# Depthwise 3x3 stages moved from VectorE to TensorE, fed by shifted copies that DMAs from ScalarE's queue make

## The chip, the cores and the metric

One core of a Trainium2 chip runs the whole program once. The metric is the device time of that execution in microseconds (us). Every tensor is float32. In what follows TensorE, VectorE, ScalarE, GpSimd and SyncE are the engines that a profile calls PE, DVE, ACT, POOL and SP; PEld is TensorE's weight load.

## What is computed

The input is 16 images of 256 channels, 32x32 pixels. Four blocks follow one another, each with a normalised copy of x and a residual sum. The two that matter here, cut to their core:

```python
# every block: GroupNorm of x first (groups of 8 channels), x = x + block(norm(x))
# L2: depthwise 3x3 -> BatchNorm -> ReLU -> prune -> 1x1 conv -> BatchNorm -> ReLU -> prune
y[c, h, w] = sum(dw_w[c, i, j] * xn[c, h + i - 1, w + j - 1] for i in range(3) for j in range(3))
# L3 (deformable conv): the same depthwise form, then LayerNorm over channels, GELU,
# one projection to offsets and a mask; xproj = in_w(xn); bilinear samples of xproj, out_w
```

L0 is a channel attention, L1 ("dyn") a 3x3 convolution whose weights depend on the pixel. The deformable part of L3 becomes, per image, 18 rows of tap weights (VectorE builds them), written to DRAM and read back as bands, and matmuls on those bands.

## The kernel before

Channels lie on the 128 partitions, in K = 2 halves (`k`) of 1024 pixels. Each engine has one in-order program. `run` (line 370 on) walks b from -1 to 16 and weaves three streams of work at every b: `side(b+1)` takes an image through L0, L1, dyn, L2, pw, L3, ln, om; `taps(b)` builds that image's 18 weight rows; `sample(b-1)` samples and projects the image before it in four quarters. `weave` puts the pieces in the order of hand-written numbers: `STEP` gives each stage its place (gn0 -3, L0 3, L1 19, dyn 28, L2 39, pw 48, L3 52, ln 63, om 68, sparse 76, end 80), and every `yield` names the place of what follows. So an engine's order is fixed when the program is built, and a piece that waits holds back all that stand after it.

The pieces around the change, in stage L2: VectorE takes channel statistics (`group_norm`, line 783 on), GpSimd the power, ScalarE writes the normed image into `xp`, a tile with a border of zeros (L1260). `first_tap` (L1268) makes tap 0 on ScalarE, `depthwise` (L812) the other eight on VectorE, one instruction of 1024 elements for each tap and half; L1315 is the ReLU. Then VectorE takes a maximum (L886), masks the pointwise weights (L891), TensorE multiplies (L502), ScalarE evicts (L1320), VectorE takes the next maximum (L896). Stage L3 repeats norm and depthwise, copies the normed image without its border into `acc` (L1326), TensorE makes `xproj` from it (L591), VectorE evicts that (L914); ln subtracts a mean (L921), takes a square root and a reciprocal (L925), and om makes offsets (L613, L935) and a softmax (L945 to L952, `Exp` at L1350).

A weight row u is a "build" on VectorE (L1140, L1149: 1, 3 or 5 instructions), a "sum" on TensorE (L666 to L668), a "row copy" on ScalarE (L1372, L1375) into a ring of two, and eight DMAs from SyncE (L458). `BUILD_AT` and `SUM_AT` place them. Four waits tie them:

```python
wait(ve, s_wrow, at - 1)                # build u waits for the row copy of u-2
wait(pe, s_wrow, at)                    # sum u waits for the row copy of u-1
wait(ac, s_w2[r], 16 * YB * (at // RING))  # row copy u: the DMAs of row u-2 have landed
ac.wait_ge(s_sum, at + 1)
```

A quarter of sampling is two parts of 32 matmuls each (L691, four column strips of 16 weights side by side), each evicted by ScalarE (L1388); the second part waits for the eviction of the first. Its projection is L702 and L703, and SyncE loads the next quarter's bands (L414, L417) after the second part. `SAMPLE_AT`, `SECOND_AT`, `EVICT_AT` and `PROJECT_AT` place them: in L2 the parts stand at 41 and 42, the evictions at 42.1 and 43.5, the projection at 44.5; in L3 at 54, 55, 55.1, 57.2 and 57.6.

Of the kernel before, what the change touches and what calls it, by code (L numbers as in the profile page):

```python
# [13 lines left out]
P = 128  # L14
# [36 lines left out]
ROW = JB * BLOCK  # L51
PAIR = C + CG
# [12 lines left out]
for _name, _after, _steps in (("L1", "L0", 16), ("dyn", "L1", 9), ("L2", "dyn", 11), ("pw", "L2", 9), ("L3", "pw", 4),  # L65
# [40 lines left out]
for _name, _n in (("q_bias", K), ("dw2_b", K), ("bn1_g", K), ("bn1_b", K), ("bn1_m", K), ("bn1_v", K),  # L106
                  ("pw_b", K), ("bn2_g", K), ("bn2_b", K), ("bn2_m", K), ("bn2_v", K), ("dw3_b", K),
                  ("ln_g", K), ("ln_b", K), ("out_b", K), ("t_gamma", 1), ("t_beta", 1),
                  ("dw2", K * TAPS), ("dw3", K * TAPS), ("b2", K * TAPS)):
    COLS[_name] = (_at, _n)  # L110
    _at += _n
# [18 lines left out]
def build(nc, x_in, weights_in, wout_in, w2x_in, cols_in, rows_in, consts_in, out, batches=B):  # L130
    ctx = ExitStack()
    with ctx:
# [17 lines left out]
        wout = sb("wout", [P, 4, C])  # L150
        w2x = sb("w2x", [P, K, TAPS, P])
# [4 lines left out]
        xp = sb("xp", [P, K, H + 2, W + 2])  # L156
        qx = sb("qx", [P, K * (H + 2) * (W + 2)])
        work = sb("work", [P, 4 * N])
# [61 lines left out]
        ident = cst_("ident")  # L220

# [32 lines left out]
        s_dw0 = sem("s_depthwise_first_tap")  # L254
        s_w = sem("s_kernel_psum")
        s_wu = sem("s_kernel_used")
        s_dw = sem("s_depthwise_done")
# [6 lines left out]
        s_flat = sem("s_normed_unbordered")  # L264
# [63 lines left out]
        N_LOAD = 6  # L328
# [7 lines left out]
        def rows_of(t3, k, half):  # L336

            return t3[:, k, 1 + half * HR:1 + (half + 1) * HR, 1:1 + W]

# [34 lines left out]
        def _(sp):  # L374
# [13 lines left out]
            sp.dma_start(wout[:, :, :].rearrange("p g n -> p (g n)"), wout_in).then_inc(s_load, 16)  # L388

# [101 lines left out]
        def _(pe):  # L491
# [16 lines left out]
            def side(f):  # L508
# [4 lines left out]
                pe.wait_ge(s_norm, f * 4 + 1)  # L513
                for j in range(4):
                    product(4 + j, lambda k: wt("w0", k, j // 2 * P, P), lambda k: rows_of(xp, k, j % 2), s_q)
# [35 lines left out]
                pe.wait_ge(s_norm, f * 4 + 2)  # L551
                for h in range(2):
                    product(4 + h, lambda k: wt("w1", k), lambda k: rows_of(xp, k, h), s_t1)
                for h in range(2):
                    yield STEP["L1"] + 5
                    product(6 + h, lambda k: wt("wv", k, 0, P), lambda k: rows_of(xp, k, h), s_xv)
# [3 lines left out]
                product(6, lambda k: wt("wv", k, P, P), lambda k: rows_of(xp, k, 0), s_xv)  # L560
                yield STEP["L1"] + 8
                pe.wait_ge(s_tr, f + 1)
                product(4, lambda k: wt("wv", k, P, P), lambda k: rows_of(xp, k, 1), s_xv)
# [12 lines left out]
                group_stats(f * 5 + 4, 4)  # L576
                yield STEP["pw"]
                pe.wait_ge(s_h, f * 2 + 2)
# [7 lines left out]
                yield STEP["L3"] + 5  # L586
                pe.wait_ge(s_flat, f * 2 + 2)

                for t in range(TILES):
                    for k in range(K):  # L590
                        mm = pe.matmul(bank(4 + t // 2, C, t % 2 * C), acc[:, k, t * P:(t + 1) * P],  # L591
                                       wt("in_w", k), start=(k == 0), stop=(k == K - 1))
                    if t % 2:
                        mm.then_inc(s_xpr, 1)
                        yield STEP["L3"] + 6 + t // 2

                yield STEP["ln"]
                pe.wait_ge(s_xprs, f * TILES + TILES)
                pe.wait_ge(s_dw3, f * 2 + 2)
# [22 lines left out]
                pe.matmul(ps[0:1, 2, 16:16 + P], runs[:, 0:1], ident, start=True, stop=True).then_inc(s_row, 1)  # L622

# [106 lines left out]
        def _(ve):  # L730
# [3 lines left out]
            vec.memset(xp[:, :, :, :], 0.0).then_inc(s_zero, 1)  # L734
# [42 lines left out]
            def side(f):  # L777
# [28 lines left out]
                def depthwise(dst, w, start, before):  # L806

                    ve.wait_ge(s_dw0, before + 2)
                    for tap in range(1, TAPS):
                        for k in range(K):  # L810
                            o = dst[:, k, :].rearrange("p (h w) -> p h w", h=H)
                            last = vec.scalar_tensor_tensor(out=o, in0=shifted(xp, k, tap // 3, tap % 3),  # L812
                                                            scalar=col(w, k * TAPS + tap), in1=o,
                                                            op0=ALU.mult, op1=ALU.add)
                            if tap == TAPS - 1:
                                last.then_inc(s_dw if w == "dw2" else s_dw3, 1)
                            else:
                                link(last)
                        if tap % 2 == 0:
                            yield start + tap // 2  # L820

# [62 lines left out]
                ve.wait_ge(s_h, f * 2 + 2)  # L884
                for k in range(K):
# [21 lines left out]
                yield STEP["L3"] + 4  # L907
                yield from depthwise(q, "dw3", STEP["L3"] + 4, f * 4 + 2)
                for t in range(TILES):
                    if t % 4 == 0:  # L910
                        yield STEP["L3"] + 8 + t // 4
                    if t % 2 == 0:
                        ve.wait_ge(s_xpr, f * 4 + t // 2 + 1)
# [321 lines left out]
        def _(ac):  # L1235
# [18 lines left out]
            def side(f):  # L1254
                def group_norm(i, start):
# [3 lines left out]
                    for k in range(K):  # L1259
# [352 lines left out]
```

## Time and profile before

| | |
|---|---|
| median of 3 runs | 5759.23 us (5756.94 to 5770.14) |
| span of the profiled execution | 5755.0 us |
| busy: VectorE, TensorE, ScalarE | 4584.3 (80%), 3462.7 (60%), 1678.5 us (29%) |
| mean granted TensorE clock | 0.787 |
| DMA, mean over the span | 97 GB/s |
| share of the chain that ended last | VectorE 60%, TensorE 19%, ScalarE 10% |

A row of a time line tells when an instruction, or a run of like ones (x16), began, how long it took altogether, and in brackets how long its engine had been idle and whom it waited for. "PEclk" or "clock" is the TensorE clock that was granted, 1.00 being 2.4 GHz and 0.50 being 1.2 GHz. One float32 matmul shows as two MATMUL instructions.

### The profile page before, as it was taken

To read this page: it belongs to the slowest core of one execution; us is meant where nothing else is said; L and a number is where in the kernel's file an instruction comes from. 1 tells how busy PE (TensorE), PEld (TensorE's weight loads), DVE (VectorE), ACT (ScalarE), POOL (GpSimd) and SP (SyncE) were. 2 spreads that over 40 slices of the span, in tenths; PEclk is the share of its full clock that TensorE was granted. 3 is DMA by queue.
4 is the path that set the end of the run, shared out by engine and by line. 5 is a ranking of instruction groups with operands and counts; after the bars stand their busy time and mean duration, and the time that the engine had idled before them with its cause. 6 is when DMAs were issued, how large, how long until landed. Compare 5 with 4: busy or idle time off the path is not lost.

```text
span 5755.0 us, 46802 instructions
## 1 busy us (share of the span) xinstructions
PE 3462.7 (60%) x16500; PEld 1965.5 (34%) x16500; DVE 4584.3 (80%) x5715; ACT 1678.5 (29%) x2081; POOL 422.3 (7%) x293
## 2 busy tenths in 40 slices
PE   5374666657566665656667566665756666665553
PEld 2131333334333333333333333333433333333332
DVE  5679788797987879798787978878798787879842
ACT  1232333223232322323232233323323232232320
POOL 0010100001010000101000010100101000010000
PEclk9687788878778787777878777787877878777676
DMA  9111224133332313333242322424332241332353
GB/s 407 46 30 38 83 80 126 54 109 96 93 91 70 129 52 102 94 85 112 70 130 56 96 85 80 126 58 113 90 92 89 74 126 52 103 97 86 100 154 108
DMA packets 619835, 558.31 MB, mean 97 GB/s; under 512 B 463760, under 2 KB 545680, under 8 KB 615632
## 3 DMA queue, kind: packets, MB, share of 16 engines
q1 hardware_dynamic: 615616, 547.85, 31.5%
q0 software_dynamic: 3984, 7.45, 0.5%
q8 instruction: 131, 2.15, 0.2%
q14 instruction: 104, 0.85, 0.0%
HBM read 279.33 MB, written 275.78 MB: 96 GB/s over the span
## 4 chain that ended last, share of the span: by engine, by line
DVE 60%; PE 19%; ACT 10%; issue 6%; POOL 2%; DMA 1%; SPq 1%; DVEq 0%; POOLq 0%; ACTq 0%
DVE spread L1149 10%; DVE partial L1140 9%; PE ps L502 6%; DVE qx L812 5%; DVE spread L1140 5%; DVE work L812 5%; DVE work L874 4%; PE ps L613 4%; DVE work L865 3%; PE ps L570 3%; DVE stats L783 2%; DVE work L925 2%; PE ps L666 1%; ACT haty L1248 1%; ACT hatx L1248 1%
## 5 line engine op out<-in xcount | busy, mean ns | idle before, releaser
L666 PE MATMUL ps<-spread,cst 128*128 128x448 f32 x576 | 362.7, 718 | 479.5 <-DVE spread L1149 451.4
L1149 DVE TENSOR_TENSOR spread<-spread,partial 128x1344 f32<-128x1344 f32 x384 | 625.2, 1628 | 13.2
L570 PE MATMUL ps<-work,w2x 128*128 128x512 f32 x1152 | 540.6, 607 | 117.0 <-DVE work L865 105.9
L1140 DVE TENSOR_TENSOR partial<-haty,hatx 128x1344 f32<-128x1344 f32 x384 | 596.3, 1553 | 5.6
L1140 DVE TENSOR_TENSOR spread<-haty,hatx 128x1344 f32<-128x1344 f32 x288 | 445.9, 1553 | 126.2 <-ACT qx L1297 112.4
L691 PE MATMUL ps<-band,near 128*16 128x96 f32 (+1 forms) x8192 | 328.2, 336 | 279.7 <-ACT samp L1388 203.7
L1372 ACT ACTIVATE partial<-spread 128x128 f32<-128x128 f32 x288 | 124.7, 433 | 1249.5 <-PE ps L668 1249.5
L1260 ACT ACTIVATE xp<-x,small 128x1024 f32<-128x1024 f32 x128 | 152.2, 1237 | 1123.9 <-POOL small L1413 1123.9
L865 DVE SCALAR_TENSOR_TENSOR work<-ps,cols,qx 128x512 f32<-128x512 f32 x576 | 406.5, 747 | 62.4 <-PE ps L570 51.6
L502 PE MATMUL ps<-qx,work 128*128 128x512 f32 x512 | 262.8, 673 | 268.1 <-DVE work L891 267.4
L702 PE MATMUL ps<-samp,wout 128*128 128x256 f32 x1024 | 276.7, 418 | 202.5 <-ACT samp L1388 202.5
L691 PEld LDWEIGHTS ps<-band,near 128*16 128x16 f32 x8192 | 265.8, 125 | 348.3 <-ACT samp L1388 216.1
L812 DVE SCALAR_TENSOR_TENSOR work<-xp,cols,work 128x1024 f32<-128x1024 f32 x256 | 327.5, 1284 | 62.2 <-ACT work L1268 54.2
L502 PE MATMUL ps<-xp,wts 128*128 128x512 f32 x640 | 319.9, 645 | 85.0 <-ACT xp L1260 62.5
L570 PEld LDWEIGHTS ps<-work,w2x 128*128 128x128 f32 x1152 | 204.7, 189 | 447.3 <-DVE work L865 305.8
L1409 POOL TENSOR_TENSOR small<-small,cst 128x2 f32<-128x2 f32 (+1 forms) x80 | 139.1, 1738 | 2871.2 <-DVE small L799 2871.2
L812 DVE SCALAR_TENSOR_TENSOR qx<-xp,cols,qx 128x1024 f32<-128x1024 f32 x256 | 327.5, 1285 | 14.6 <-ACT qx L1268 6.1
L874 DVE TENSOR_TENSOR work<-work 128x1024 f32<-128x1024 f32 x256 | 313.5, 1225 | 8.7
L666 PEld LDWEIGHTS ps<-spread,cst 128*128 128x128 f32 x576 | 113.1, 230 | 606.6 <-DVE spread L1149 545.4
L667 PE MATMUL ps<-spread,cst 128*128 128x384 f32 x576 | 307.2, 622 | 0.0
L668 PE MATMUL ps<-spread,cst 128*128 128x384 f32 x576 | 303.6, 617 | 0.0
L702 PEld LDWEIGHTS ps<-samp,wout 128*128 128x128 f32 x1024 | 216.0, 213 | 253.8 <-ACT samp L1388 207.0
(237 smaller groups left out, 5522.0 us busy)
## 6 DMA issues: line engine op xcount, KB each, us to landing
band<-taps_dram SPq DMA_DIRECT2D x512, 384.0 KB
taps_dram<-partial SPq DMA_DIRECT2D x1280, 48.0 KB
near<-img_dram SPq DMA_DIRECT2D x256, 128.0 KB
img_dram<-band SPq DMA_DIRECT2D x6, 4096.0 KB, 40.8
taps_dram<-band SPq DMA_DIRECT2D x6, 4096.0 KB, 87.1
om_now<-om SPq DMA_DIRECT2D x32, 576.0 KB, 11.1
om_dram<-om SPq DMA_DIRECT2D x32, 576.0 KB, 11.9
x<-x_in SPq DMA_DIRECT2D x16, 1024.0 KB, 9.1
```

The lines of the kernel that those rows point to most:

```text
L502: mm = pe.matmul(bank(b), w(k), t(k), start=(k == 0), stop=(k == K - 1))
L570: pe.matmul(bank(4 + i % 4), w2x[:, half, tap, :], tr[:, h * HALF:(h + 1) * HALF], start=True, stop=True).then_inc(s_w, 1)
L666: pe.matmul(bank(1, inner), ident, parts[:, 1, :], start=True, stop=False)
L667: pe.matmul(bank(1, inner - HG), ident, parts[:, 0, HG:E * HG], start=False, stop=False)
L668: pe.matmul(bank(1, inner - HG, HG), ident, parts[:, 2, 0:inner - HG], start=False, stop=True).then_inc(s_sum, 1)
L691: mm = pe.matmul(o, near[:, j, g * CG:(g + 1) * CG], band[:, :, j, a:z, g, :], start=(c == 0 and j == 0), stop=(j == JB - 1), skip_group_c ...
L702: pe.matmul(o, wout[:, gq, half * P:(half + 1) * P], samp[:, gq, :], start=(gq == 0), stop=False)
L812: last = vec.scalar_tensor_tensor(out=o, in0=shifted(xp, k, tap // 3, tap % 3), scalar=col(w, k * TAPS + tap), in1=o, op0=ALU.mult, op1=AL ...
L865: vec.scalar_tensor_tensor(out=t.rearrange("p (h w) -> p h w", w=W), in0=bank(4 + i % 4).rearrange("p (h w) -> p h w", w=W), scalar=col("b ...
L874: vec.tensor_tensor(o, o, work[:, 3 * N:4 * N], ALU.add).then_inc(s_v, 1)
L1140: return build(vec.tensor_tensor(o, haty[:, :, 3 * i:3 * i + 3, :].rearrange("p e j a -> p j e a"), cells, ALU.mult))
L1149: done = build(vec.tensor_tensor(total, total, spare, ALU.add))
```

## The change

In both stages the depthwise convolution leaves VectorE. `xp` keeps one zero column between rows (pitch 33, 1058 elements a half). For each half `k`, strip `j` of 32 channels and horizontal shift `dx`, one DMA copies 32 partitions of 1056 elements (4224 bytes a partition, 132 KB) to partitions 32*dx of a tile `copies(k, j)`: 12 DMAs a half, 24 a stage, all issued from ScalarE's program (`replicate`). In L2 all 24 stand together behind the norm, at place 42; in L3 12 at 55 and 12 at 56. TensorE's `depthwise` multiplies 96 partitions (three shifts of 32 channels) by a stacked diagonal of 96x32 weights, for three row taps, four strips and two halves of the rows: 24 matmuls of 480 or 512 columns for a half `k`, 48 a stage, at places 44 and 45 in L2, 58 and 60 in L3. ScalarE evicts each half in two pieces of 512 with bias, and ReLU in L2. `HALVES` takes half 1 before half 0. The unbordered copy of L3 is made in two pieces (`flat`), the second after the first four tiles of `xproj`, which now stand at place 56, before the depthwise. Eight of the 18 builds and their sums get other places. A seventh load (`wdw`, 768 KB) is added at the start, and the Pool queue's scratch is set to 8192.

```diff
+PITCH = W + 1
+SHIFT = H * PITCH
+ROW_TAPS = (1, 0, 2)
+HALVES = (1, 0)
...
-    + [STEP["L2"] + 3.5, STEP["pw"] + 1, STEP["pw"] + 2, STEP["L3"] + 3.5, STEP["ln"], STEP["ln"] + 2, STEP["ln"] + 3,
-       STEP["om"] - 0.1, STEP["om"] + 4]
-SUM_AT = [at + 1.6 for at in BUILD_AT]
+    + [STEP["L2"] + 3.5, STEP["L2"] + 4, STEP["L2"] + 4.5, STEP["L2"] + 5, STEP["pw"] + 1, STEP["L3"] + 3.5, STEP["L3"] + 6,
+       STEP["L3"] + 7, STEP["ln"] + 2]
+SUM_AT = [at + 1.6 for at in BUILD_AT[:9]] + [STEP["L2"] + 4.6, STEP["L2"] + 4.8, STEP["L2"] + 5.5, STEP["L2"] + 6.5, STEP["pw"] + 2.6,
+    STEP["L3"] + 5.1, STEP["L3"] + 7, STEP["L3"] + 8.2, STEP["ln"] + 3.6]
...
+            if k == 0:
+                return work[:, j * SHIFT:(j + 1) * SHIFT]
+            return (qx[:, 0:SHIFT], qx[:, SHIFT:2 * SHIFT], keys[:, 0:SHIFT], mout[:, 0:SHIFT])[j]
...
+                for turn, k in enumerate(HALVES):
+                    yield STEP["L2"] + 5 + turn
+                    depthwise(f, 0, k)
...
-                yield STEP["L3"] + 5
-                pe.wait_ge(s_flat, f * 2 + 2)
-
+                yield STEP["L3"] + 4
                 for t in range(TILES):
+                    pe.wait_ge(s_flat, f * 4 + t // 4 * 2 + 2)
...
+                for turn, k in enumerate(HALVES):
+                    yield STEP["L3"] + 6 + 2 * turn
+                    pe.wait_ge(s_xprs, f * TILES + 4 * turn + 4)
+                    depthwise(f, 1, k)
...
+            def depthwise(f, stage, k):
+
+                pe.wait_ge(s_rep[k], (2 * f + stage + 1) * COPIES)
+                for h in range(2):
+                    b = 4 + 2 * HALVES.index(k) + h
+                    for i in ROW_TAPS:
+                        first, last = max(h * HR, 1 - i), min((h + 1) * HR, H + 1 - i)
+                        for j in range(4):
+                            rows_in = copies(k, j)[0:3 * QUAD].rearrange("p (h w) -> p h w", w=PITCH)
+                            o = ps[j * QUAD:(j + 1) * QUAD, b, (first - h * HR) * W:(last - h * HR) * W]
+                            mm = pe.matmul(o.rearrange("p (h w) -> p h w", w=W), wdw[0:3 * QUAD, stage, k * 4 + j, i, :],
+                                           rows_in[:, first + i - 1:last + i - 1, 0:W],
+                                           start=(i == ROW_TAPS[0]), stop=(i == ROW_TAPS[-1]), skip_group_check=True)
+                    mm.then_inc(s_dwp, 1)
...
-                yield STEP["L2"] + 4
-                yield from depthwise(acc, "dw2", STEP["L2"] + 4, f * 4)
...
-                yield STEP["L3"] + 4
-                yield from depthwise(q, "dw3", STEP["L3"] + 4, f * 4 + 2)
+                yield STEP["L3"] + 5
...
+                def replicate(i, turns):
+
+                    for turn in turns:
+                        k = HALVES[turn]
+                        ac.wait_ge(s_norm, f * 8 + 2 * i + turn + 1)
+                        for j in range(4):
+                            for dx in range(3):
+                                ac.dma_start(copies(k, j)[dx * QUAD:(dx + 1) * QUAD, :],
+                                             xp[j * QUAD:(j + 1) * QUAD, k, dx:dx + SHIFT]).then_inc(s_rep[k], 16)
...
-                first_tap(acc, "dw2", None, 3)
-                yield STEP["pw"] - 2
+                wait(ac, s_omd, f * 112)
+                replicate(2, (0, 1))
+                for turn, k in enumerate(HALVES):
+                    yield STEP["L2"] + 5.1 + turn
+                    for h in range(2):
+                        ac.wait_ge(s_dwp, f * 8 + (h + 3 if turn else 2))
+                        act.activation(q[:, k, h * HALF:(h + 1) * HALF], bank(4 + 2 * turn + h), ACT.Relu,
+                                       bias=col("dw2_b", k), scale=col("bn1_g", k)).then_inc(s_h, 1)
...
+                for turn in range(2):
+                    yield STEP["L3"] + 3 + turn
+                    replicate(3, (turn,))
+                    ac.wait_ge(s_norm, f * 8 + 8)
+                    wait(ac, s_xpr, f * 4 + 2 * turn)
+                    for k in range(K):
+                        act.activation(flat[:, k, :].rearrange("p (h w) -> p h w", w=W), inner(k, turn * HR, HR), ACT.Copy)\
+                            .then_inc(s_flat, 1)
```

## Rows read from the trace of the kernel before

**Rows 1.** The page, busy us of each engine (share of the span).
```profile
PE 3462.7 (60%) x16500; PEld 1965.5 (34%) x16500; DVE 4584.3 (80%) x5715; ACT 1678.5 (29%) x2081; POOL 422.3 (7%) x293
```

**Rows 2.** The chain in order of time: start us, us, what. One image's beginning.
```profile
2058.59 7.32 PE ps L502 x16
...
2399.93 7.31 PE ps L502 x16
```

**Rows 3.** Time line of VectorE, one image: start us, us, engine, line, op, tiles, [idle before].
```profile
2155.00 4.35 DVE L1132 TENSOR_TENSOR hatx<-hatx,om 128x4032 f32<-128x4032 f32 x1
...
2164.07 20.97 DVE L812 SCALAR_TENSOR_TENSOR work<-xp,cols,work 128x1024 f32<-128x1024 f32 x16 [3.13 <-ACT work L1268]
...
2186.35 2.35 DVE L886 TENSOR_REDUCE small<-qx 128x1 f32<-128x1024 f32 x2 [1.31 <-ACT qx L1315]
...
2194.89 1.56 DVE L1140 TENSOR_TENSOR spread<-haty,hatx 128x1344 f32<-128x1344 f32 x1
...
2202.73 2.35 DVE L896 TENSOR_REDUCE small<-work 128x1 f32<-128x1024 f32 x2
...
2220.51 20.97 DVE L812 SCALAR_TENSOR_TENSOR qx<-xp,cols,qx 128x1024 f32<-128x1024 f32 x16
...
2252.65 2.48 DVE L921 TENSOR_TENSOR qx<-qx,ps 128x512 f32<-128x512 f32 x4
...
2270.72 6.55 DVE L925 RECIPROCAL work<-work 128x1024 f32<-128x1024 f32 x1
...
2298.18 2.13 DVE L945 TENSOR_REDUCE red<-om 128x128 f32<-128x1152 f32 x1
...
2304.75 2.15 DVE L950 TENSOR_REDUCE red<-om 128x128 f32<-128x1152 f32 x1 [2.79 <-ACT om L1350]
```

**Rows 4.** Time line of ScalarE, the same image.
```profile
2159.44 2.38 ACT L1260 ACTIVATE xp<-x,small 128x1024 f32<-128x1024 f32 x2 [44.02 <-POOL small L1413]
...
2163.94 0.57 ACT L1388 ACTIVATE samp<-ps 128x512 f32<-128x512 f32 x1
...
2170.74 1.03 ACT L1375 ACTIVATE partial<-ps 128x448 f32<-128x448 f32 x1
...
2214.31 2.38 ACT L1260 ACTIVATE xp<-x,small 128x1024 f32<-128x1024 f32 x2 [7.31 <-POOL small L1413]
...
2302.26 1.28 ACT L1350 ACT_TABLE_LOAD   x1
```

**Rows 5.** Time line of TensorE, the same image.
```profile
2109.35 7.03 PE L570 MATMUL ps<-work,w2x 128*128 128x512 f32 x16
...
2164.57 3.19 PE L691 MATMUL ps<-band,near 128*16 128x96 f32 x64 [7.49 <-ACT samp L1388]
...
2167.69 1.44 PE L666 MATMUL ps<-spread,cst 128*128 128x448 f32 x2
...
2170.25 1.89 PE L702 MATMUL ps<-samp,wout 128*128 128x256 f32 x8
...
2189.69 10.18 PE L502 MATMUL ps<-qx,work 128*128 128x512 f32 x16 [14.96 <-DVE work L891]
...
2233.78 5.34 PE L591 MATMUL ps<-wts,work 128*128 128x256 f32 x24
...
2296.89 1.73 PE L691 MATMUL ps<-band,near 128*16 128x96 f32 x64
```

**Rows 6.** By line: SyncE's DMA issues, ns min/median/max of one.
```profile
L482 SPq DMA_DIRECT2D out<-res x64: 378/458/1827, 753.0 to 5686.4; - x64
...
L414 SPq DMA_DIRECT2D band<-taps_dram x512: 751/752/1184, 605.0 to 5662.1; - x171
```

**Rows 7.** Two stretches: PE, PEld, DVE, ACT, POOL busy, clock, DMA share, GB/s.
```profile
2176.00:2186.00 10.00, 0.00 (x0) 0.00 (x0) 8.86 (x7) 2.12 (x2) 0.00 (x0) 0.64 0.85 215
...
2318.00:2328.00 10.00, 6.38 (x22) 4.96 (x21) 5.10 (x14) 9.97 (x11) 0.00 (x0) 0.79 1.03 396
```

**Rows 8.** The chain, first image alone, the end of its stage L2.
```profile
168.38 2.36 DVE small L886 x2
```

More of the change, by code:

```diff
@@ L127, with build @@
 NCST = _at
-def build(nc, x_in, weights_in, wout_in, w2x_in, cols_in, rows_in, consts_in, out, batches=B):
+def build(nc, x_in, weights_in, wout_in, wdw_in, w2x_in, cols_in, rows_in, consts_in, out, batches=B):
     ctx = ExitStack()
@@ L155, in build @@
         x = sb("x", [P, K, N])
-        xp = sb("xp", [P, K, H + 2, W + 2])
+        xp = sb("xp", [P, K, NORMED])
         qx = sb("qx", [P, K * (H + 2) * (W + 2)])
-        work = sb("work", [P, 4 * N])
+        work = sb("work", [P, 4 * SHIFT])
         big = sb("big", [P, TILES, C])
@@ L220, in build @@
         ident = cst_("ident")
+        flat = big[:, TILES // 2:, :].rearrange("p t c -> p (t c)").rearrange("p (k n) -> p k n", k=K)
         ps = ctx.enter_context(nc.psum_tensor("ps", [P, 8, 512], F32))
@@ L253, in build @@
         s_xvz = sem("s_xv_border_zeroed")
-        s_dw0 = sem("s_depthwise_first_tap")
+        s_rep = [sem(f"s_shifted_copies_{i}") for i in range(K)]
+        s_dwp = sem("s_depthwise_psum")
+        s_flat = sem("s_normed_unbordered")
         s_w = sem("s_kernel_psum")
         s_wu = sem("s_kernel_used")
-        s_dw = sem("s_depthwise_done")
         s_h = sem("s_h_relu")
@@ L804, in group_norm @@
                     yield from moments(lambda k, h: x[:, k, h * HALF:(h + 1) * HALF], K, stat, start)
[L806 to L820, printed above, removed]
                 yield STEP["gn0"]
@@ L880, in side @@
                 yield from group_norm(f * 5 + 4, STEP["L2"])
-                yield STEP["L2"] + 4
-                yield from depthwise(acc, "dw2", STEP["L2"] + 4, f * 4)
                 yield STEP["pw"] - 1
-                ve.wait_ge(s_h, f * 2 + 2)
-                for k in range(K):
+                for turn, k in enumerate(HALVES):
+                    ve.wait_ge(s_h, f * 4 + 2 * turn + 2)
                     last = vec.tensor_reduce(small[:, 44 + k:45 + k], q[:, k, :], AX.X, ALU.max)
@@ L1580, in two @@
         return v.reshape(K, P).T
-    def taps(w):
-        return w.reshape(K, P, TAPS).transpose(1, 0, 2).reshape(P, K * TAPS)
+    wdw = np.zeros((4, QUAD, 2, K * 4, 3, QUAD), np.float32)
+    for stage, w in enumerate((a["L2_conv_dw_w"], a["L3_conv_dw_w"])):
+        for c in range(QUAD):
+            wdw[:3, c, stage, :, :, c] = w.reshape(K * 4, QUAD, 3, 3)[:, c].transpose(2, 0, 1)
     c = {"q_bias": two(a["L0_conv_bias"]), "dw2_b": two(a["L2_conv_dw_b"]), "pw_b": two(a["L2_conv_pw_b"]),
@@ L1587, in lay_out @@
          "out_b": two(a["L3_conv_out_b"]), "t_gamma": a["L1_conv_gn_gamma"].reshape(P, 1),
[L1588 removed]
+         "t_beta": a["L1_conv_gn_beta"].reshape(P, 1),
          "b2": b2}
```

74 lines of the change are left out of this document (35 added, 39 removed).

## The prediction, made before the changed kernel was run

> **What bounds the kernel now.** I read the page first, for shares. VectorE is busy 4584.3 us of 5755.0 and TensorE 3462.7 [rows 1]; no engine fills the span, so what counts is the order of work. The chain in order of time then shows a repeating pattern: the attention products begin at 2058.59 and again at 2399.93 [rows 2], so one image costs 341.3 us, 15 times over (b = 0 to 14, the first without sampling). The first image's side work stands alone before that, the last image's taps and sampling alone behind it. The time lines of the three engines through one period give the rest. VectorE's busy time, 4584.3/16 = 287 us an image, holds two depthwise runs of 20.97 us [rows 3], 41.9 us together, and both are on the chain. In L2 the norm ends at 2161.8 [rows 4] and the first maximum starts at 2186.35 [rows 3]: 24.5 us, in which VectorE does nothing but taps. In L3 the run starts at 2220.51 behind weight builds; the builds at ln and ln+2 lie between it and the reciprocal at 2270.72 [rows 3].
>
> **Prices.** A build of five instructions is 7.85 us (2194.89 to 2202.73 [rows 3]). One float32 matmul of 512 columns takes 7.03/8 = 0.88 us at the full clock, 583 columns per us [rows 5]; so a sum (1216 columns) is 2.1 us, and 2.5 where the clock rises within it (2167.69 to 2170.25 [rows 5]). A row copy is 1.3 us, 1.03 for its longer part and the start of the shorter ahead of it [rows 4]. A sampling part is 3.2 us at 1.2 GHz and 1.73 at 2.4 [rows 5], its eviction 0.6 [rows 4], a projection 4.3.
>
> The depthwise on TensorE: a half k streams 1504 columns twice, in each of four strips, 12032 in all. Bounds: with no overlap of strips 12032/583 = 20.6 us; with full overlap 5.2. The sampling part is the nearest row: 3584 columns in four strips in 1.73 us [rows 5], 2070 per us, which makes 5.8. Its matmuls are 112 columns on average and pay their start more often than mine of 500, so I take 5.3, and about double at the low clock. The Trainium skill has a rule that speaks against it: in "TensorE: Matmul & The Clock Gate", section "Measured speedup vs the span model", three column tiles of 512 columns gave only 2.38 times. By the page four tiles would give an estimated 3.2 times and a half 6.5 us. The trace does not agree: the sampling row gives 2070/583 = 3.55 times.
>
> The copies: 24 issues a stage on ScalarE's program. The trace has no issue from ScalarE. SyncE's cost 0.38 to 0.46 us for a plain form (least and median) and 0.75 for the bands [rows 6]; below that, nothing excludes an issue that hardly holds ScalarE. Mine have few, long rows, nearest to the plain store, so 0.45: 10.8 us for 24, 5.4 for 12. The data, 24 x 135 KB = 3.24 MB, take 15.1 us at 215 GB/s and 8.2 at 396 [rows 7]. The Trainium skill, "DMA: Bandwidth & Descriptors", section "Issuing engines are not separate DMA queues", calls the issue time of a DMA usually small beside the DMA itself. Here the rows make them alike, and the issue is the one that an in-order engine feels. By that rule the forecast would move to the cheap-issue case below.
>
> **L2, step by step (times of the old trace).** Half 1 is normed at 2160.6. ScalarE issues 24 DMAs to 2171.4. Behind them on ScalarE stands the eviction of the first sampling part, so it ends at 2172.0, not 2164.5. TensorE's second part waits for it: 2175.2. Then the sum of row 9 to 2177.7, its copy to 2179.0, and only then may VectorE build row 11 (the wait of u on u-2); it had built 9 and 10 by 2165.6 and idles 13 us. Build 11 ends at 2186.85. TensorE meanwhile: sum 10, depthwise of half 1 until 2186.4 (its copies landed by about 2172). Sum 11 to 2188.95, projection to 2193.25, depthwise of half 0 to 2198.55, eviction 2199.35, maximum and mask 2201.35 against 2189.5 before: 12 us later, with builds 10, 11 and 12 (20.4 us) done instead of none. In pw TensorE is now warm (7.1 us instead of 10.18 [rows 5]) and one build remains, where two stood: the next maximum starts at 2210.1 instead of 2202.73, **7.4 us later**. SyncE's band load moves behind the late part, and the DMAs of row 10 behind it: they land near 2204, and the copy of row 12 on ScalarE waits there ahead of the pw evictions. I cost this at nothing: those evictions end near 2209.3, under build 13. Ten more microseconds of backlog would show.
>
> **L3 to ln.** Norm of half 1: 2215.5 + 7.4 = 2222.9 [rows 4]. Twelve issues to 2228.3, two flat copies 1.2, eviction 0.6: 2230.1. TensorE: second part cold to 2233.3, four tiles of xproj (24 instructions take 5.34 us [rows 5], so 16 take 3.6) to 2236.9. ScalarE's other twelve issues end at 2235.5, under that; flat copies to 2238.1; four tiles to 2241.7; then in a row sum 14, projection, depthwise, sum 15, depthwise, sum 16: 2.1 + 4.3 + 5.3 + 2.1 + 5.3 + 2.1 = 21.2, so 2262.9, and the mean 3.6 more. VectorE subtracts at 2266.5 instead of 2252.65. But two builds (15.7 us) no longer follow: subtraction, square, variance, root take 8.0, so the reciprocal starts at 2274.5 instead of 2270.72, **3.8 later**. In om the sum between the two runs of products is gone (-2.1), and the row copy that held ScalarE's table load until 2302.26 [rows 4] is gone: the load needs to wait for nothing then, and the second reduction, now 2304.75 [rows 3], gains 1.8. Net **-0.1 us** an image. The 41.9 us taken off VectorE come back as ScalarE's issue time and a packed TensorE; VectorE then idles over 90 us of 341.
>
> **Sum.** Fourteen full periods: -1. The first image, alone: the norm of half 1 ends 25.7 us before its maximum (168.38 [rows 8]); issues 5.4, landing 3, depthwise 9 (cold at first) and 5.3, eviction and half a maximum 2.0, so about -1 there and -4 with a warm pw and shorter L3: -5. Period b = 0 has no sampling between: -6. Last image: builds 10 to 12 go before the waits for bands, -6, an estimate from the same prices. The seventh load at 396 GB/s: +2. Together -16: span 5739. The median of before lies 4.2 above the span of its profile, so 5743.
>
> **Rivals.**
> (1) Issues on ScalarE are dear. 24 + 12 of them are on the chain, so each 0.1 us is 3.7 us an image, 55 us in all; my gain of 16 us is gone at 0.48 us an issue. At 0.60, 5825; at the bands' 0.75, with L3's second twelve then late too, 13 x 15 = 195: 5940. This is the case on the slower side. For it: ScalarE's program must also run its waits. Against: 0.38 exists.
> (2) Issues are cheap. At the least of 0.38: 5703; at next to nothing 9 us in L2 (landing and TensorE bind) and 6 in L3: 5743 - 225 = 5518.
> (3) Strips overlap less, by the page's ratio or worse. Three of the four halves are on the chain: +1.2 x 3 x 15 = 54, 5797; with no overlap 15.3 x 3 x 15 = 690, 6430. For it: mine contract over 96 partitions with 32 columns of weights; against: the sampling row.
> (4) The DMA backlog holds the copy of row 12: some 5 us an image, 5818.
> (5) VectorE is the bound and all 41.9 us go: 5755 - 630, 5130. Against: the norm waits, and 54 us a period in which VectorE is idle already.
>
> **How the numbers follow.** Forecast 0.38 (5695 to 5790: faster 0.21, within 0.2% 0.10, slower 0.07); (1) 0.18, (2) 0.23, (3) 0.11, (4) 0.06, (5) 0.04. This gives faster 0.21 + 0.23 + 0.04 = 0.48, same 0.10, slower 0.42; 0.2% (12 us) is what a measurement of this kernel can tell from no change. The range for 8 in 10 leaves out (5), the far end of (2) and the dear ends of (1) and (3): 5590 to 5880.
>
> **What would show it.** Right: the eviction of the first L2 part 8 to 11 us later than before, directly behind 24 issues; VectorE idle about 13 us ahead of build 11, waiting for a row copy; TensorE without gaps from the second part to the mean in L3; a half of the depthwise 5.2 to 5.8 us; periods of 341 us. Wrong: issues of 0.2 or 0.7 us, halves over 7 us, periods under 335 or over 347, TensorE waiting for the copies to land, or ScalarE waiting in a row copy for DMAs.

## The result, and the profile after

The changed kernel took 5942.02 us (median of 4 runs, 5939.44 to 5944.52), the kernel before beside it 5761.89: ratio 1.0313, 95% interval 1.0301 to 1.0326. It is 3.1% slower, 199 us over the forecast of 5743 and above the whole range (to 5880). The profiled execution has a span of 5937.5 us.

The page of the changed kernel: busy time of each engine, then the shares of the chain that ended last, and one image's period in the chain in order of time (start us, us, what). The last group answers to [rows 2], the first to [rows 1].

```profile
PE 3726.1 (63%) x19572; PEld 2036.1 (34%) x19572; DVE 3914.3 (66%) x5203; ACT 1664.4 (28%) x2145; POOL 410.3 (7%) x293
...
DVE 38%; PE 33%; ACT 10%; ACTq 6%; issue 5%; SPq 3%; POOL 3%; DMA 2%; DVEq 0%; POOLq 0%
```

```profile
2111.83 7.40 PE ps L523 x16
...
2466.82 7.40 PE ps L523 x16
```

VectorE lost 670 us of work, as the change says, and its share of the chain fell from 60% to 38%. The period grew from 341.3 to 355.0 us. What is new in the chain is "ACTq", ScalarE's DMA issues. Here is where they stand; the time line of ScalarE in L2 and in L3 (start us, us, engine, line, op, tiles, [idle before <- whom it waited for]):

```profile
2212.76 2.37 ACT L1279 ACTIVATE xp<-x,small 128x1024 f32<-128x1024 f32 x2 [44.01 <-POOL small L1446]
2214.08 3.74 ACTq L1290 DMA_DIRECT2D qx<-xp  x6
2217.85 1.90 ACTq L1290 DMA_DIRECT2D keys<-xp  x3
2219.78 1.90 ACTq L1290 DMA_DIRECT2D mout<-xp  x3
2221.72 7.68 ACTq L1290 DMA_DIRECT2D work<-xp  x12
2229.49 0.60 ACT L1421 ACTIVATE samp<-ps 128x512 f32<-128x512 f32 x1 [14.36 <-issue]
...
2253.46 0.45 ACT L1405 ACTIVATE partial<-spread 128x128 f32<-128x128 f32 x1 [6.31 <-DMA taps_dram<-partial]
...
2281.72 3.72 ACTq L1290 DMA_DIRECT2D qx<-xp  x6
...
2290.45 0.58 ACT L1421 ACTIVATE samp<-ps 128x512 f32<-128x512 f32 x1
```

And the line that issues them, by its instructions (ns min/median/max of one), with the time to landing:

```profile
L1290 ACTq DMA_DIRECT2D work<-xp x384: 514/612/2234, 152.6 to 5485.4; - x192
...
DMA to landing us min/median/max: 2.3/2.5/7.8
```

An issue takes 0.61 us, and 24 of them take 15.4 us from the first to the eviction behind them (2214.08 to 2229.49): 0.64 each. That eviction started at 2163.94 before [rows 4]; counted from the norm (2159.44, now 2212.76, so 53.32 later), it is 12.2 us late. VectorE and TensorE of the changed kernel, the rows on which the step-by-step comparison below rests:

```profile
2238.13 1.56 DVE L1159 TENSOR_TENSOR spread<-haty,hatx 128x1344 f32<-128x1344 f32 x1 [19.34 <-ACT partial L1408]
...
2268.86 2.34 DVE L918 TENSOR_REDUCE small<-work 128x1 f32<-128x1024 f32 x2
...
2329.01 2.48 DVE L940 TENSOR_TENSOR qx<-qx,ps 128x512 f32<-128x512 f32 x4 [9.94 <-PE ps L523]
...
2339.75 6.55 DVE L944 RECIPROCAL work<-work 128x1024 f32<-128x1024 f32 x1 [6.79 <-ACT work L1369]
...
2371.46 2.15 DVE L969 TENSOR_REDUCE red<-om 128x128 f32<-128x1152 f32 x1 [2.30 <-ACT om L1383]
```

```profile
2252.12 5.25 PE L659 MATMUL ps<-work,wdw 96*32 96x512 f32 x48
...
2294.20 5.12 PE L614 MATMUL ps<-wts,big 128*128 128x256 f32 x16
2300.62 3.72 PE L614 MATMUL ps<-wts,big 128*128 128x256 f32 x16 [1.30 <-ACT big L1354]
...
2325.38 3.60 PE L523 MATMUL ps<-qx,cst 128*128 128x512 f32 x8
2332.63 6.36 PE L523 MATMUL ps<-work,cst 128*128 128x512 f32 x8 [3.66 <-ACT work L1365]
```

Three things are to be seen: build 11 waits 19.34 us for a row copy that stands behind the issues; a half of the depthwise costs 5.25 us; and the variance product takes 6.36 us where the mean product, the same form, takes 3.60.

### The profile page after: what moved, and what is told of

Read it like the earlier page. It is cut to its first block, busy times and chain, and to the rows that moved or that the text cites. A ratio compares the mean times of both kernels' runs of the same rounds, so it can differ in the third digit from the quotient of the medians.

```text
span 5937.5 us, 53298 instructions
## 1 busy us (share of the span) xinstructions
PE 3726.1 (63%) x19572; PEld 2036.1 (34%) x19572; DVE 3914.3 (66%) x5203; ACT 1664.4 (28%) x2145; POOL 410.3 (7%) x293
## 4 chain that ended last, share of the span: by engine, by line
DVE 38%; PE 33%; ACT 10%; ACTq 6%; issue 5%; SPq 3%; POOL 3%; DMA 2%; DVEq 0%; POOLq 0%
PE ps L523 8%; ACTq L1290 6%; DVE spread L1168 6%; DVE partial L1159 5%; PE ps L659 5%; DVE work L898 4%; PE ps L638 4%; DVE spread L1159 3%; DVE work L889 3%; PE ps L591 3%; PE ps L742 2%; PE ps L614 2%; PE ps L706 2%; DVE stats L823 2%; PE ps L731 2%
## 5 line engine op out<-in xcount | busy, mean ns | idle before, releaser
L1168 DVE TENSOR_TENSOR spread<-spread,partial 128x1344 f32<-128x1344 f32 x384 | 598.3, 1558 | 13.2
L706 PE MATMUL ps<-spread,cst 128*128 128x448 f32 x576 | 343.0, 682 | 337.8 <-DVE spread L1168 273.6
L638 PE MATMUL ps<-wts,work 128*128 128x432 f32 x512 | 223.1, 601 | 154.8 <-ACT work L1375 154.8
L519 PE MATMUL ps<-small,cst 128*128 128x4 f32 (+1 forms) x160 | 40.9, 326 | 427.5 <-DVE small L830 416.4
L1408 ACT ACTIVATE partial<-ps 128x448 f32<-128x448 f32 x288 | 294.4, 1022 | 0.0
L707 PE MATMUL ps<-spread,cst 128*128 128x384 f32 x576 | 285.5, 583 | 0.0
L708 PE MATMUL ps<-spread,cst 128*128 128x384 f32 x576 | 278.1, 570 | 0.0
```

Of the source, the lines that this page charges most:

```text
L638: mm = pe.matmul(bank(4 + t % 4, OM), acc[:, k, t * P:(t + 1) * P], wt("om_w", k), start=(k == 0), stop=(k == K - 1))
L706: pe.matmul(bank(1, inner), ident, parts[:, 1, :], start=True, stop=False)
L1168: done = build(vec.tensor_tensor(total, total, spare, ALU.add))
```

## The experiments

My theory (A) after the result: the issues on ScalarE are the loss, since everything behind them in ScalarE's order (eviction, second sampling part, row copies, builds) moves with them. The rivals: the TensorE work of the depthwise itself (theory B in the first expectations), copies that land late (C), the DMAs' own backlog, and the low clock of single products. Of these, C is answered by the changed kernel's own trace: over the whole run TensorE waited for the copies once, 12.9 us.

### The issues: taken to SyncE, doubled, taken to GpSimd

`replicate` is called from SyncE's `side`, at the places that it had on ScalarE, and no longer from ScalarE's:

```diff
             def side(f):
+                yield STEP["L2"] + 3
+                wait(sp, s_omd, f * 112)
+                replicate(sp, f, 2, (0, 1))
...
+                for turn in range(2):
+                    yield STEP["L3"] + 3 + turn
+                    replicate(sp, f, 3, (turn,))
...
-                wait(ac, s_omd, f * 112)
-                replicate(2, (0, 1))
...
-                    replicate(3, (turn,))
```

> The same copies, issued from SyncE's program instead of ScalarE's. Theory A (ScalarE's issue time, 0.64 us each from one start to the next, holds the sampling eviction and row copies behind it): the eviction of the first L2 part comes back to right behind the norm, the second maximum of L2 starts 10 to 15 us earlier, L3 gains 7 to 10 more, so 17 to 25 us an image and 5550 to 5680 us in all. Theory B (TensorE's packed order is the bound, the issues hide under it): less than 5 us an image, above 5860. Theory C (the landing of the copies is late): no change, TensorE waits for the DMAs.

Measured: 5748.57 us (5740.63 to 5763.72), ratio 0.9979 (0.997 to 0.9989), 193 us less than the changed kernel. The direction is A's, the size is not. ScalarE's time line in L2 shows where the rest went:

```profile
2167.77 1.45 ACT L1342 ACTIVATE qx<-ps,cols 128x512 f32<-128x512 f32 x2 [3.83 <-PE ps L674]
2189.40 0.43 ACT L1407 ACTIVATE partial<-spread 128x128 f32<-128x128 f32 x1 [20.18 <-DMA taps_dram<-partial]
```

and SyncE's, why:

```profile
2160.32 7.59 SPq L374 DMA_DIRECT2D work<-xp  x12
2167.95 6.46 SPq L444 DMA_DIRECT2D band<-taps_dram  x8
2174.45 2.48 SPq L447 DMA_DIRECT2D near<-img_dram  x4
2176.98 22.70 SPq L494 DMA_DIRECT2D taps_dram<-partial  x32
```

The row-11 copy waits for the DMAs of row 9, and those stand behind 24 copies and 12 band loads. The issues were gone from one queue, and a part of their cost, some 150 us as the runs below show, was back in another.

Twice the issues in L2, from ScalarE as in the changed kernel, same bytes:

```diff
+                                parts = 2 if i == 2 else 1
+                                n = SHIFT // parts
+                                for part in range(parts):
+                                    ac.dma_start(copies(k, j)[dx * QUAD:(dx + 1) * QUAD, part * n:(part + 1) * n],
+                                                 xp[j * QUAD:(j + 1) * QUAD, k, dx + part * n:dx + (part + 1) * n])
```

> Each of the 24 copies of L2 is cut into two DMAs of half the bytes; L3 is left alone. Theory A: 24 more issues at 0.5 to 0.64 us on the chain, 12 to 15 us an image, 6130 to 6190 us. Theory B and C: within 1% of the changed kernel, 5900 to 5990, since the bytes and TensorE's work are the same.

Measured: 6153.61 us (6152.91 to 6154.3), ratio 1.0683 (1.0661 to 1.0704). 24 more issues an image cost 211 us, 13.2 an image, 0.55 us each, as A expected; by time line they pass at 0.64 (24 `work` issues in 15.35 us). So 0.55 of the 0.64 us of an issue is on the path. With the run above, which takes the issues off ScalarE, this is the direct evidence for A.

The same 24 from GpSimd, which was idle 93% of the time (`replicate` called from its program at the same places):

> The changed kernel with all 24 copies of a stage issued by GpSimd, which is busy 7% of the time, in place of ScalarE; nothing else changes, SyncE's queue neither. Theory A (the price is that of 0.6 us of issue each on the engine, wherever that is): no queue order problem as with SyncE; the second-half copies land about when they do now, ScalarE is free for the evictions of sampling and the row copies: 5600 to 5720. Theory B (an issue costs GpSimd 1 us or more): 24 us or more a stage before the second half can start, over 5850.

Measured: 5730.81 us (5726.18 to 5737.54), ratio 0.9952 (0.9936 to 0.9967): 211 us less than the changed kernel, and 11 above the end of A's range. By its line, issues took

```profile
L374 POOL DMA_DIRECT2D work<-xp x384: 489/489/506, 151.2 to 5285.8; - x192
```

so 0.49 us on GpSimd, 0.59 on SyncE (median of the same copies there), 0.61 on ScalarE. The row-11 copy still waited 13.63 us for DMAs, with SyncE's twelve band loads ahead of row 9.

### The order of ScalarE around the issues

Only the eviction of the first sampling part goes ahead of the norm, hence ahead of the 24 issues:

```diff
-EVICT_AT = [..., (STEP["L2"] + 3.1, STEP["L2"] + 4.5), (STEP["L3"] + 3.1, STEP["L3"] + 5.2),
+EVICT_AT = [..., (STEP["L2"] + 2.9, STEP["L2"] + 4.5), (STEP["L3"] + 2.9, STEP["L3"] + 5.2),
```

> Only the place of one eviction in L2 and one in L3 changes: ahead of the norm on ScalarE, not behind the issues. Theory A: the second sampling part and the sum of row 9 run while the DMAs are issued, the row copy stands directly behind them: about 7 us in L2 and 3 to 4 in L3 of each image, 5770 to 5800 us. Theory B: the packed TensorE work is shorter by the part and the sum as well, so it expects the same sign here, but in L3 nothing: about 5830. Theory C: no change.

Measured: 5905.98 us (5903.12 to 5908.83), ratio 1.0253 (1.0232 to 1.0273). 36 us gained where 140 to 170 were expected: a miss. TensorE and ScalarE in this run:

```profile
2221.54 0.42 ACT L1405 ACTIVATE partial<-spread 128x128 f32<-128x128 f32 x1
...
2279.41 6.14 PE L614 MATMUL ps<-wts,big 128*128 128x256 f32 x16 [7.83 <-ACT big L1354]
```

The second part does run early, but the row copy that build 11 waits for stands behind the 24 issues too (2221.54), and in L3 the unbordered copy behind twelve; TensorE, idle 7.83 us, then runs xproj in 6.14 us. The eviction was one of several things behind the issues, not the cause.

### The depthwise on TensorE

Two of the three row taps are left out, so the depthwise result is another one; the copies and their issues stay:

```diff
-ROW_TAPS = (1, 0, 2)
+ROW_TAPS = (1,)
```

> Two of the three row taps of the depthwise are left out on TensorE, 3.5 us of each 5.25 us half; the copies stay. Theory A with my walk (three of four halves on the chain, the first of L2 beside a build of VectorE): 9 to 11 us an image, 5760 to 5800 us. Were the issues the only thing that counts: 5900 or more. Theory B: all four halves and the warm clock count, 5700 to 5760.

Measured: 5845.54 us (5841.35 to 5849.73), ratio 1.0148 (1.0128 to 1.0168). A half fell from 5.25 to 1.93 us and the kernel by 97 us, 6.0 an image, where three halves on the path would give 10.0. In L2 something else then ends last; TensorE's time line:

```profile
2219.76 1.93 PE L659 MATMUL ps<-work,wdw 96*32 96x512 f32 x16
2226.81 1.83 PE L706 MATMUL ps<-spread,cst 128*128 128x448 f32 x2 [5.12 <-ACT partial L1408]
```

Sum 12 waits 5.12 us for the row-11 copy, which waits for DMAs. Here the backlog ends later than TensorE's work, which hides it in the changed kernel (the first run of the next section). Even with two thirds of TensorE's depthwise gone, the kernel stays slower than before.

### The backlog: where the band load stands

A new list places SyncE's load of the next quarter's bands (it stood at `EVICT_AT[quarter][1] + 0.5`). In L2 it goes to 7.5, behind the DMAs of row 12, in L3 to 8.9.

```diff
+BAND_AT = [EVICT_AT[0][1] + 0.5, STEP["L2"] + 7.5, STEP["L3"] + 8.9, EVICT_AT[3][1] + 0.5]
...
-                    yield EVICT_AT[quarter][1] + 0.5
+                    yield BAND_AT[quarter]
```

On the changed kernel (issues on ScalarE):

> The changed kernel with its 24 copies still issued by ScalarE; only the load of the next quarter's bands is moved behind the DMAs of rows 9 to 12 in L2 and of rows 14 to 16 in L3. Row copies wait 129.5 us there for DMAs of taps, 8.1 an image, which the prediction costed at nothing. Theory A (the loads ahead of row 9 in SyncE's queue hold them): 4 to 8 us an image go, 5815 to 5880. Theory B (the rows' own 32 DMAs are the queue): less than 1 us an image, 5925 to 5945.

Measured: 5985.38 us (5983.67 to 5987.08), ratio 1.0392 (1.0372 to 1.0413), so 43 us slower than the changed kernel. Neither case. VectorE's second half of the first maximum, changed kernel and then this run:

```profile
2258.26 1.22 DVE L908 TENSOR_REDUCE small<-qx 128x1 f32<-128x1024 f32 x1 [3.23 <-ACT qx L1339]
```

```profile
2271.31 1.22 DVE L909 TENSOR_REDUCE small<-qx 128x1 f32<-128x1024 f32 x1 [3.22 <-ACT qx L1340]
```

From the start of the norm it is 45.50 us in the one (2212.76) and 45.47 in the other (2225.84), though ScalarE's wait of 6.31 us for DMAs is gone. So that wait cost nothing in the changed kernel. What the edit costs is a wait of the sampling for its bands, here at the head of L3:

```profile
2299.18 3.19 PE L732 MATMUL ps<-band,near 128*16 128x96 f32 x64 [8.33 <-DMA near<-img_dram]
```

TensorE's waits for `near` grew from 85.7 us (6 times) in the changed kernel to 206.3 us (21 times). Not all of it is on the path: in the image shown it is 24.95 us from L3's norm to the sum behind `xproj`, against 23.72 in the changed kernel. Of the 43 us, 21 lie behind the second reduction of the last image, where sampling stands alone (from it to the end of the span 378.0 us in the changed kernel, 398.7 here); the rest is some 3 us in each of seven periods.

With SyncE's issues, where the wait was 20 us, the same edit:

> SyncE issues the 24 copies of each stage, and the load of the next quarter's bands is moved behind the DMAs of rows 9 to 12 in L2 and of rows 14 to 16 in L3. Theory A (SyncE's queue order makes the 20.2 us wait of the row-11 copy in the run before this, because 24 copies and 12 loads of bands stand ahead of row 9): the loads took 8.9 us there (2167.95 to 2176.9), so that wait falls to 8 to 12 us, a period of 341.4 to 330 to 333, the time 5560 to 5640. Theory B (the DMA engines are full, not the queue): the wait stays over 17 us and the time within 5720 to 5760. Against both: the sampling of L3 waits for its bands, the time stays and the wait moves there.

Measured: 5653.39 us (5648.34 to 5663.54), ratio 0.9821 (0.9805 to 0.9837), 95 us less than the run with the load at its old place, though 13 over A's range. The wait of the row-11 copy is gone, and 6.77 us of waiting for bands stand at the head of L3. The last image's sampling is longer here too. Hence the place between rows 10 and 11, `STEP["L2"] + 5.3`:

> As the run with SyncE's issues and late bands (5653), but in L2 the load of the bands stands between the DMAs of row 10 and row 11, not behind row 12. Theory A (two things share SyncE's queue: the rows, which the row copies wait for, and the bands, which the first sampling part of L3 waited 6.8 us an image for): both waits go, 5540 to 5600. Theory B (the row-11 DMAs, now behind the bands, hold the copy of row 13, or the bands are held by the DMA engines and not by their place): 5630 to 5700.

Measured: 5598.26 us (5596.18 to 5598.84), ratio 0.9717 (0.9701 to 0.9733), as A expected. TensorE's waits for `near` over the whole run, the late place and then this one (us, times, longest):

```profile
PE ps L747 <- DMA near<-img_dram: 207.5, 21, 20.7
```

```profile
PE ps L747 <- DMA near<-img_dram: 92.9, 6, 20.2
```

Of the 55 us between the two runs, 22 are in the last image (from the start of its norm in L2 to the end 540.4 and 518.2 us); a full period went from 334.5 (in some images 331.2) to 331.1 us.

The same place with GpSimd's issues:

> As the run with GpSimd's issues (5731), with the same place of the band load as the run before this. There the row-11 copy waited 13.6 us an image for the DMAs of row 9. Theory A (twelve band loads ahead of row 9 are that wait): it falls under 4 us and the time comes to 5500 to 5600, at or under that of SyncE's issues, since the copies' issue took 0.48 us each there and keeps SyncE's queue free. Theory B (the copies' packets fill the DMA engines): over 5680.

Measured: 5607.18 us (5606.68 to 5607.67), ratio 0.9734 (0.9714 to 0.9753): 7 us over A's range and 124 under the run with the old place. Row copies still waited 5.2 us an image for DMAs (78.5 us, 15 times). A full period is 331.1 us with either engine's issues; the 9 us between the two runs are in the first image. In this order of work it was the place in SyncE's queue that mattered, and hardly the engine that issues.

### The clock

Eight matmuls on constants, 3.5 us, between mean and variance in the changed kernel; nobody reads what they make:

```diff
+                for i in range(8):
+                    pe.matmul(bank(7, 256, 256), cst_("mean256"), cst[:, 0:256], start=True, stop=True)
```

> The changed kernel, with eight matmuls of 256 columns on constants (3.5 us, into an unused bank corner that nobody reads) between the mean and the variance of L3, where TensorE is idle for 3.66 us and then runs the variance product in 6.36 us in place of the 3.6 us that the prediction took. Theory A (the product is slow since TensorE stood idle ahead of it and was given the lower clock): the product falls to 3.6 us, 2.7 us an image, 5885 to 5915. Theory B (the product is slow for its operands): it stays at 6.3 us and the time at 5935 to 5950.

Measured: 5901.29 us (5900.6 to 5904.34), ratio 1.0246 (1.0227 to 1.0264), as A expected: 41 us less than the changed kernel, for more work. TensorE in this run, and below it the variance product's stretch by windows (us, PE, PEld, DVE, ACT, POOL busy, clock, DMA share, GB/s), changed kernel first, then this run:

```profile
2315.35 3.62 PE L628 MATMUL ps<-cst 128*128 128x256 f32 x16
2319.18 3.70 PE L523 MATMUL ps<-work,cst 128*128 128x512 f32 x8 [0.21 <-ACT work L1367]
```

```profile
2333.00:2339.00 6.00, 6.00 (x9) 2.42 (x9) 0.00 (x0) 1.57 (x2) 0.00 (x0) 0.58 0.42 92
```

```profile
2319.00:2323.00 4.00, 3.82 (x9) 1.82 (x10) 0.50 (x1) 2.18 (x4) 0.00 (x0) 1.00 0.59 123
```

The clock granted to the product is 1.00 in place of 0.58, and it takes 3.70 us in place of 6.36. What TensorE did in the 3.66 us ahead of it decides that, not its operands.

### Best version, and two controls

On the run with SyncE's issues and the bands between rows 10 and 11: the two evictions ahead of the norm, and the projections later. L2's goes behind the depthwise of half 0, L3's into the gap between mean and variance, where real work now does what the filler did:

```diff
-PROJECT_AT = [STEP["dyn"] + 1.5, STEP["L2"] + 5.5, STEP["L3"] + 5.6, STEP["om"] + 8.5]
-RESULT_AT = [STEP["dyn"] + 3.1, STEP["pw"], STEP["ln"] - 1, STEP["end"]]
+PROJECT_AT = [STEP["dyn"] + 1.5, STEP["L2"] + 6.3, STEP["ln"] + 0.5, STEP["om"] + 8.5]
+RESULT_AT = [STEP["dyn"] + 3.1, STEP["pw"], STEP["ln"] + 2.5, STEP["end"]]
```

> As the first of these, and besides: the eviction of the first sampling part ahead of the norm in L2 and L3, the projection of L2's quarter behind the depthwise of half 0 and that of L3's quarter between the mean and the variance. Theory A (behind the issues TensorE's packed order sets L2 and L3: projection 4.4 us in each, of which 3.2 us in L2 and 4.4 us in L3 are on the path): 5 to 8 us an image less than the first of these, 5430 to 5510. Theory B (VectorE's builds are the bound and TensorE's order is not): less than 2 us an image less.

Measured: 5506.32 us (5504.92 to 5509.95), ratio 0.9561 (0.9545 to 0.9577), as A expected, 92 us or 5.7 an image less than the run that it builds on. There the variance product took 5.40 us behind the same idle 3.66. TensorE at ln in this run:

```profile
2151.74 3.60 PE L539 MATMUL ps<-qx,cst 128*128 128x512 f32 x8
2155.17 1.89 PE L758 MATMUL ps<-samp,wout 128*128 128x256 f32 x8
...
2159.49 3.60 PE L539 MATMUL ps<-work,cst 128*128 128x512 f32 x8
```

The product is 1.8 us shorter, and the projection (4.3 us) has left the packed run ahead of the mean.

Would placement alone have given this to the kernel before? Its evictions and L3's projection moved in the same way, depthwise still on VectorE:

> The kernel before, depthwise still on VectorE, with the two placement edits of the best version that it can take: evictions of the first sampling part ahead of the norm in L2 and L3, and L3's projection between the mean and the variance. Theory A (the gain to 5506 comes from the depthwise on TensorE; there VectorE sets the path in both stages, so TensorE's order is off it): 5735 to 5765. Theory B (the placement alone gives it): under 5700.

Measured: 5753.37 us (5748.77 to 5757.22), ratio 0.9986 (0.9976 to 0.9996). No: 7 us. The place of the band load was not moved in this control, but the trace of the kernel before leaves it little to gain. No row copy waits for DMAs there, and the only wait of TensorE for bands is this one (us, times, longest):

```profile
PE ps L691 <- DMA near<-img_dram: 76.0, 5, 19.1
```

What the new places of eight builds give by themselves was not tested. And the best version with GpSimd's issues:

> As the run with the late projections and the early evictions (5506), with all copies issued by GpSimd in place of SyncE. Theory A (with the issues off ScalarE the path runs through VectorE's builds and TensorE's order, and who issues no longer matters): within 20 us of 5506. Theory B (SyncE's queue is still what orders L2): 30 us or more less, under 5475.

Measured: 5560.43 us (5557.19 to 5561.88), ratio 0.9652 (0.9635 to 0.9669), 54 us slower than with SyncE's. A miss for both. TensorE's first depthwise instructions in L2, SyncE's issues and then GpSimd's:

```profile
2077.62 0.62 PE L675 MATMUL ps<-qx,wdw 96*32 96x512 f32 x2 [2.73 <-DMA mout<-xp]
```

```profile
2101.55 1.07 PE L669 MATMUL ps<-qx,wdw 96*32 96x512 f32 x2 [4.50 <-DMA mout<-xp]
```

TensorE waits longer for the copies although they are issued faster: GpSimd's take 4.3 us to land (median), SyncE's 2.6. The depthwise starts 12.89 us after the start of the norm (2088.66, 2101.55) against 11.13 (2066.49, 2077.62), 1.8 us later. After the longer wait the half runs at a granted clock of 0.52 (2101 to 2107) where the other had 0.66 (2078 to 2083), and ScalarE's eviction of it starts 21.43 us after the norm (2110.09) against 18.14 (2084.63). That is 3.3 us an image; a full period is 327.7 against 324.3. The rest of the 54 us is mainly in the first image, whose L2 norm is followed by the next image's after 315.2 and 303.8 us.

Sharing the DMA engines with the rows is not the main reason for the later landing. In L2 of the first image no rows are written yet; the landing of its 24 copies (window 140 to 190), GpSimd's issues and then SyncE's:

```profile
DMA to landing us min/median/max: 2.5/4.3/6.4
```

```profile
DMA to landing us min/median/max: 2.4/2.6/3.0
```

With GpSimd's issues it grows from 2.5 us for the first copy to 6.4 for the last. The 3.24 MB moved at 195 GB/s in one case (146 to 158) and 204 in the other (146 to 160). So an explanation that fits, not tested further: the data move at some 200 GB/s whoever issues them, and copies that are issued at a faster rate queue up. Other DMAs come on top only where there are many: in the first run with GpSimd's issues, beside the band loads, single copies took up to 17.9 us.

## Why the prediction was wrong, point by point

Times of the changed kernel below are those of its trace less 53.32 us, which puts the starts of the two kernels' L2 norms in one place; rows are shown as they stand in the trace.

- **The price of an issue, the step that failed first.** I took 0.45 us from the plain store to DRAM [rows 6]. It is 0.61 us, and 0.64 from start to start. L2's first eviction starts at 2176.2 and not 2171.4 (+4.8), and L3's twelve issues take 7.6 and not 5.4 (+2.2): 7 us of the 13.8 an image by which the period missed 341. The row was the wrong neighbour: the same copies take 0.59 on SyncE, so it is these copies that are dearer than a store, hardly the engine. A nearer row was in the trace of the kernel before, SyncE's loads of 128 KB into a tile (ns min/median/max of one):

```profile
L417 SPq DMA_DIRECT2D near<-img_dram x256: 528/594/1420, 611.5 to 5664.7; - x128
```

  My rival 1 had the slope right, 550 us for each us of an issue. With 0.59 the forecast would have been 5820, slower than the kernel before; with the measured 0.64 it is 0.19 x 550 = 105 us more, 5848. That is still inside my range, so this step alone does not give 5942.
- **The clock, a term not in the sum, the step that failed next.** I priced the products of L3 warm. The variance product took 6.36 us for 3.6 (+2.7), the first four tiles of xproj 5.12 for 3.6 (+1.5; clock 0.69), and the sum of row 9 was 1 us over (clock 0.67). That is 5 us an image here; in other runs the variance product took 5.40. The filler run shows the first of these; the others are read from the rows alone. Before, xproj had VectorE's depthwise beside it and its own length did not count; the prediction said that TensorE becomes the path there and then did not ask at what clock it comes out of each wait. Rows of the kernel before showed the price, the first eight instructions of xproj behind a part at the low clock, and the mean product behind an idle 5.06 us:

```profile
2224.64 2.94 PE L591 MATMUL ps<-wts,work 128*128 128x256 f32 x8
...
2244.18 5.12 PE L502 MATMUL ps<-qx,cst 128*128 128x512 f32 x8 [5.06 <-DVE big L914]
```

  At the rate of [rows 5] the eight take 1.8 us, and the product takes 3.6.
- **The table load.** Predicted free to go ahead (-1.8). It still stands behind the subtraction:

```profile
2368.97 1.28 ACT L1383 ACT_TABLE_LOAD   x1 [1.98 <-DVE om L965]
```

  and VectorE waits 2.30 us where it waited 2.79 [rows 3]: 0.5 gained and not 1.8 (+1.3).
- **The order of L2: right.** ScalarE's issues stand ahead of the eviction, the second part runs at the low clock in 3.19 us, and VectorE is idle ahead of build 11 (19.34 us; I said 13, and the 4.8 and 1 us from above make most of the rest). The second maximum came at 2215.5, predicted 2210.1.
- **Depthwise on TensorE: right.** 5.3 taken, 5.25 measured; four strips overlap almost fully. Rival 3 falls, and for this shape the page's ratio with it: by the Trainium skill, "TensorE: Matmul & The Clock Gate", section "Measured speedup vs the span model", three column tiles gave 2.38 times. Here 20.6 us without overlap against 5.25 is 3.9 times for four strips.
- **The packed run of L3: right.** From the end of xproj to the mean 21.2 us were predicted; it ran from 2304.17 to 2325.38.
- **The backlog at nothing: right here, by luck of its cover.** ScalarE waits 6.31 us in a row copy and it costs nothing (the late-band run), since TensorE's order ends later. It is the copy of row 11, behind the DMAs of row 9, where I had named row 12; and I named the cover as the evictions under build 13, where it was TensorE's depthwise. With the issues on SyncE a row copy waits 20 us, and the cover is gone. The wait of a row copy was one of my signs of being wrong; it came, as did a period over 347, but only the period told of the loss.
- **VectorE is not the bound: right.** It lost 670 us and the kernel got slower. Rival 2 (cheap issues, down to 5518) was not met by taking the issues off ScalarE alone: that gave 5749 and 5731, and only other places for the band load (5598) and for evictions and projections (5506) came near it.

Added up: issues 7.0, clock 5.2, table load 1.3, which is 13.5 of the 13.8 us of a full period. The whole miss of 199 us is not simply 15 such periods. From L2 norm to L2 norm the first period did not grow (317.2 to 317.3 us), where I had taken 11 us off for the first image and b = 0; the second grew by 0.7, the other thirteen by 9.5 to 14.0, 167 in all; the last image, from its L2 norm to the end, by 13.0, where I had taken 6 off. The terms for the first and last image were thus too good by some 30 us. The last image's L2 is as dear as the others' (68.1 us from its norm to that of L3, 54.9 before). In the first image L2 gained 3.2 us (47.6 for 50.8 from norm to norm), and L3 lost 4.9 up to the subtraction (39.9 for 35.0), where I had a gain.

The Trainium skill, "DMA: Bandwidth & Descriptors", section "Issuing engines are not separate DMA queues", says of the issue time that it is "usually small relative to the DMA itself". For one copy here it is a quarter: 0.61 us of issue beside 2.5 us to landing. But 24 stand in a row, their transfers overlap, and the in-order engine pays each issue.

## What to carry to other kernels

Count DMA issues as instructions of the engine that issues them: 24 small copies are 15 us in which nothing behind them in that program runs, and taking them to another queue moves the question to what stands behind them there. Take the price of an issue from the nearest kind of DMA (here 0.59 us for loads into a tile, not 0.45 for stores), and say what the forecast becomes at the other bound when the break-even lies between them. When work moves to TensorE and TensorE becomes the path, price each product by what TensorE does just before it. Useful work put into such a gap gives back more than its own time: here 4.3 us of projection moved, and the product behind it 1.8 us shorter.

## What the runs showed of the hardware

- The same 132 KB copy (32 partitions, 4224 bytes each) costs an issue of 0.61 us on ScalarE, 0.59 on SyncE and 0.49 on GpSimd; at half the bytes ScalarE's 24 issues still took 15.35 us. So between 66 and 132 KB the price goes by the issue and not by the size.
- GpSimd's faster issues land later: 4.3 to 4.4 us in the median of three runs, against 2.5 on ScalarE and 2.5 to 2.6 on SyncE. They do so in the first image too, beside no rows, and all 24 moved at some 200 GB/s from either engine.
- 3.6 us of matmuls that nobody reads made the kernel 41 us faster, by a granted clock of 1.00 in place of 0.58 for the product behind them.
- Matmuls of 96 rows and 32 columns of weights in four column strips ran at 2290 columns per us (12032 in 5.25 us), 3.9 times the 583 of the 128-column matmuls.
